# Expert stage of a decoder layer: the dots' normed row in a PSUM bank, similarities in one bank

## Chip, cores, metric

One NeuronCore of a Trainium2 chip runs the whole kernel. The metric is the device time of one execution in microseconds (us), less being better. The engines are PE (matmul), DVE (vector), ACT (scalar), POOL (GpSimd) and SP, which here only issues DMAs.

## The reference

A decoder layer on x of 8 x 224 tokens with 512 features, fp32: self-attention with 16 heads, cross-attention over 750 context rows, and a product-key mixture of experts. Only the last is touched by the change; its core is

```python
q = jnp.einsum('bnd,de->bne', x, w_q)            # then batch norm over all tokens
sim = jnp.einsum('pbnhd,hkpd->pbnhk', q, keys)   # two halves p, 8 heads h, 128 keys k
sx, ix = jax.lax.top_k(sim[0], TOPK); sy, iy = jax.lax.top_k(sim[1], TOPK)
...                                              # top 8 of the 64 sums, indices ix*128 + iy
wd = down_embed[indices]; wu = up_embed[indices]
h = gelu_new(jnp.einsum('bnd,bnhkd->bnhk', x, wd))
h = jax.nn.softmax(scores, axis=-1) * h
out = jnp.einsum('bnhk,bnhkd->bnd', h, wu)
```

with x the layer-normed rows. Every token takes 8 experts in each of 8 heads, and an expert has a down row and an up row of 512 numbers.

## The kernel before

`build_attention` does both attentions batch by batch and leaves x2 in `acc` and its layer norm in `xn_all`, both token-major: 14 tiles (`NTF`) of 128 tokens. `build_experts` then runs the 8 heads (`HF`).

**Units.** A head has 28 units (`NV`), two per token tile. A unit treats 4 of the 8 chosen experts (`HU`) of each of the tile's 128 tokens. Its steps, by engine and line: POOL gathers 4 times 128 rows of 4 KB (down and up row side by side) into a slot of the ring `rows` of 6 units (L1769); DVE forms 4 dots of the down halves with the tile's normed row, in place, the sum going to `hidden` (L1965); ACT takes the gelu (L2042, `active`); DVE multiplies by the gate (L1976, `weight`); ACT writes 4 diagonal matrices (L2047, `diag`, room for two units); PE multiplies each by the up rows (L1819), and a tile's 8 products accumulate in one of two PSUM banks, `ps_y` or `ps_o`. After every second product `rows_used` counts up, and POOL waits on it before it reuses the slot. DVE adds a finished tile into `acc` two tiles later (L1955, `add_rows`).

**Steps.** The choice of the next heads' experts is cut into 40 steps that are interleaved with the units: `steps_in` says which steps go with which unit. From head 1 on, unit v does step v + 20 of the next head (v < 20) and step v - 8 of the one after (v >= 8). `PE_STEPS`, `DVE_STEPS` and `ACT_STEPS` hold them: PE projects queries (L1789, steps 0 to 7 and 12 to 19) and multiplies them with the keys, two tiles at a time, 7 groups for each half (`match_keys`, L1802, into `ps_t`, steps 12 to 18 and 23 to 29); DVE takes statistics of the queries (L1847), and finds the best 8 of each group (`search`: MAX8 at L1876, FIND_INDEX8 at L1879), two steps behind the product, then joins the halves (L1889 to L1899) and makes indices and gates (L1908 to L1934, steps 32 to 39). ACT normalizes the queries (L2022, steps 10 and 22).

**Order in a unit.** Each engine's queue is in order. PE: steps, then the four products. DVE: dots, `add_rows` on a tile's first unit, steps, wait for the gelu, weight. ACT: gelu, wait for the weight, diagonals, steps. The product of group g waits until search g - 2 is done, as two banks alternate; the search waits for its product through `sims_made`.

**PSUM.** All eight banks are in use: four for projected queries (`ps_s`), two for similarities (`ps_t`, called `ps_m` in `build_experts`), two for the weighted sums.

Of the kernel before, what the change touches and what calls it, by code (L numbers as in the profile page):

```python
# [14 lines left out]
ALU = mybir.AluOpType  # L15
# [59 lines left out]
AHEAD_TILES = (B - 1) * S // P // 2 * 2  # L75
# [1463 lines left out]
HF = 8  # L1539
KD = 128  # L1540
NK = 128
# [19 lines left out]
def build_experts(nc, a, out, x2_dram, x2n_dram, acc, xn_all, xn_t, w_in, keys, gamma, beta, stats, ps_q, ps_m, ps_out, ident):  # L1561
# [5 lines left out]
    with ExitStack() as ctx:  # L1567
# [51 lines left out]
        idx_here = sem("idx_here")  # L1619
        rows_in = [sem(f"rows_in{g}") for g in range(RING)]  # L1620
        rows_used = sem("rows_used")
        hidden_ready = sem("hidden_ready")
        active_ready = sem("active_ready")
        weight_ready = sem("weight_ready")
# [21 lines left out]
        def piece_of(n0, n1):  # L1646
# [3 lines left out]
            match = q_t[:, 0:2 * n * TOP * TOP].rearrange("p (s t k j) -> p s t k j", s=2, k=TOP, j=TOP)  # L1650
            return pair, match

        def group(g):
            return range(g * TPB, min(NTF, (g + 1) * TPB))

# [3 lines left out]
        for half, (p0, m0) in enumerate(((0, 12), (12, 23))):  # L1659
            for i in range(2 * QC):  # L1660
                PE_STEPS[p0 + i].append(("project", half, i))
            for c in range(QC):
                DVE_STEPS[p0 + 2 * c + 3].append(("count", half, c))
            DVE_STEPS[p0 + 10].append(("affine", half, 0))
            for g in range(NG):
                PE_STEPS[m0 + g].append(("match", half, g))
                DVE_STEPS[m0 + g + 2].append(("search", half, g))
        for k, part in ((32, 0), (33, 1), (34, 2), (35, 3)):
            DVE_STEPS[k].append(("pairs", 0, part))
        for k, part in ((36, 0), (36, 1), (37, 2), (38, 3), (39, 4)):  # L1670
# [103 lines left out]
        def _(pe):  # L1774
# [19 lines left out]
            def match_keys(head, half, g):  # L1794

                n = nth(head, half)
                pe.wait_ge(q_ready, QC * n + -(-P * TPB * (g + 1) // QN))

                if n >= 1 or g >= 2:
                    pe.wait_ge(searched, NG * n + g - 1)  # L1800
                for i in group(g):
                    mm = nc.tensor.matmul(ps_m[g % 2][:, (i % TPB) * NK:(i % TPB + 1) * NK],  # L1802
                                          q_t[:, i * P:(i + 1) * P], keys[:, half, :], start=True, stop=True)
                mm.then_inc(sims_made, 1)

# [38 lines left out]
        def _(dve):  # L1844
# [22 lines left out]
            def search(head, half, g):  # L1867
# [2 lines left out]
                dve.sem_inc(passed_dve, 1)  # L1870

                def sims(i):
                    return ps_m[g % 2][:, (i % TPB) * NK:(i % TPB + 1) * NK]

                for i in group(g):
                    nc.vector.max(best[:, half, i, :], sims(i))  # L1876
# [80 lines left out]
            def unit(h, t, s, step):  # L1957
                v = SPT * t + s
                b = v % 2
                if h == 0 and v == SPT * AHEAD_TILES:  # L1960
                    dve.wait_ge(x2_in, 32)
                dve.wait_ge(rows_in[v % RING], 16 * HU * (uses(v % RING) * h + v // RING + 1))
                for k in range(HU):
                    down = rows[:, v % RING, k, 0:D]
                    last = nc.vector.tensor_tensor_reduce(down, down, xn_all[:, t, :], 1.0, 0.0, ALU.mult, ALU.add,  # L1965
                                                          hidden[:, b, k:k + 1])
                last.then_inc(hidden_ready, 1)
                if v == 0 and h >= 1:
# [41 lines left out]
        def _(act):  # L2010
# [18 lines left out]
            def steps(head, k):  # L2029
                for stage, half, part in ACT_STEPS.get(k, ()):  # L2030
# [4 lines left out]
                    else:  # L2035
                        soften(head)

            def unit(h, t, s, step):
                v = SPT * t + s
                b = v % 2  # L2040
                act.wait_ge(hidden_ready, NV * h + v + 1)
                nc.scalar.activation(active[:, b, :], hidden[:, b, :], ACT.Gelu_apprx_tanh).then_inc(active_ready, 1)  # L2042
                act.wait_ge(weight_ready, NV * h + v + 1)

                act.wait_ge(rows_used, 2 * (NV * h + v - ND + 1 + RING))
                for k in range(HU):
                    nc.scalar.activation(diag[:, HU * (v % ND) + k, :], ident[:], ACT.Copy, scale=weight[:, b, k:k + 1])\  # L2047
                        .then_inc(diag_ready, 1)
                step()
# [7 lines left out]
                    soften(0, n0, n1)  # L2057

            first_head()
            run_heads(steps, unit, lambda: None)  # L2060


# [69 lines left out]
```

## Time and profile before

| | us |
|---|---|
| median of 3 runs | 2746.43 (2737.4 to 2747.01) |
| the profiled execution | 2732.75 |
| its span | 2730.9 |
| granted TensorE clock, mean | 0.943 of full speed |
| first gather starts | 1358.2 |

The profile is a page on one execution: busy time by engine, the span in 40 slices, DMA queues, the chain of waits that ended last, the costliest groups of instructions with what ended the idle time before them, and DMA issues. Behind the page, the trace can be asked for a stretch, a line, a tile, the waits or the order in time. Lines are those of the kernel file (L1965). In a timeline row the numbers are start and duration in us; the bracket at its end is the engine's idle time before it and what ended it, where "issue" stands for nothing that the profile shows and "remote" or "an unknown queue" for a releaser that it can't name. In the order of work, `ps_y` and `ps_o` at L1819 are the weighted sums of alternate tiles.

### The profile page before, as it was taken

What the parts mean: (1) busy time and instruction counts of PE and PEld (TensorE: products, weight loads), DVE (VectorE), ACT (ScalarE), POOL (GpSimd) and SP (SyncE); (2) the same over time, 40 slices, a digit from 0 to 9 for tenths busy, and PEclk for the clock granted to TensorE, in tenths of its full rate; (3) what the DMA queues carried; (4) which work ended last, traced back from release to release, by engine and by line L of the source; (5) the groups of instructions that cost most, each with busy time, mean ns of one, the idle gap of its engine ahead of it and who ended that gap; (6) DMA issues with size and microseconds to landing.
All of it is one profiled execution on the core that took longest, in us unless ns stands there. A gap on an engine that the chain in (4) does not pass through costs nothing.

```text
span 2730.9 us, 37792 instructions
## 1 busy us (share of the span) xinstructions
PE 2356.3 (86%) x12444; PEld 1259.1 (46%) x12444; DVE 1869.2 (68%) x5474; ACT 1176.5 (43%) x3224; POOL 1144.1 (42%) x1082
## 2 busy tenths in 40 slices
PE   8999999999999999998868888778878788876767
PEld 4565555656555565655534433333333343332323
DVE  4676777777687777768467767677775766766554
ACT  3365574736557473657223423323333332332222
POOL 3111212111121211120166576676667666577665
PEclk9999999999999999999989999989899998898889
DMA  4001001010100101011189899999999999899998
GB/s 175 30 1 37 8 8 37 1 44 1 41 4 10 36 1 43 1 60 58 58 320 364 299 369 357 349 354 345 358 352 363 351 362 358 309 359 356 355 375 330
DMA packets 161954, 521.78 MB, mean 191 GB/s; under 512 B 17248, under 2 KB 27488, under 8 KB 161760
## 3 DMA queue, kind: packets, MB, share of 16 engines
q0 software_dynamic: 129024, 469.82, 45.8%
q1 hardware_dynamic: 31152, 48.03, 5.3%
q8 instruction: 100, 1.64, 0.2%
q10 hardware_dynamic: 1584, 1.52, 0.2%
q14 instruction: 94, 0.77, 0.1%
HBM read 508.30 MB, written 11.01 MB: 190 GB/s over the span
## 4 chain that ended last, share of the span: by engine, by line
PE 20%; issue 10%; DVE 10%; another core or an unknown queue 3%; POOL 3%; DMA 3%; ACT 1%; DVEq 1%; POOLq 0%; ACTq 0%
PE ps_y L1819 7%; PE ps_o L1819 7%; DVE e_rows L1965 5%; PE ps_s L1789 3%; POOL e_rows L1769 3%; DMA e_rows<-in_experts,e_idx 3%; PE ps_t L1802 1%; ACT e_diag L2047 1%; DVE acc L1955 1%; DVE e_at L1899 1%; DVE e_best_at L1879 1%; DVEq L1903 0%; DVE q_stats L1847 0%; ACT e_q_t L2022 0%
## 5 line engine op out<-in xcount | busy, mean ns | idle before, releaser
L1769 POOL DMA_INDIRECT e_rows<-in_experts,e_idx x896 | 908.6, 1014 | 473.0 <-issue 284.6
L1965 DVE CUSTOM_DVE_ANT_0 e_rows<-e_rows,xn_all 128x512 f32<-128x512 f32 x896 | 568.6, 688 | 148.4 <-DMA e_rows<-in_experts,e_idx 112.5
L1819 PE MATMUL ps_o<-e_rows,e_diag 128*128 128x512 f32 x896 | 443.1, 642 | 149.2 <-issue 131.3
L1819 PE MATMUL ps_y<-e_rows,e_diag 128*128 128x512 f32 x896 | 434.5, 632 | 121.6 <-ACT e_diag L2047 60.4
L2047 ACT ACTIVATE e_diag<-ident_f,e_weight 128x128 f32<-128x128 f32 x896 | 286.3, 390 | 560.5 <-DVE e_weight L1976 197.1
L1819 PEld LDWEIGHTS ps_o<-e_rows,e_diag 128*128 128x128 f32 x896 | 179.8, 206 | 384.7 <-issue 362.5
L1819 PEld LDWEIGHTS ps_y<-e_rows,e_diag 128*128 128x128 f32 x896 | 178.1, 203 | 355.1 <-issue 316.1
L1133 DVE SCALAR_TENSOR_TENSOR ring<-ps_s,mask 112x750 f32<-112x750 f32 x248 | 225.0, 936 | 129.2 <-PE ps_s L624 110.1
L1359 ACT ACTIVATE ring<-ring,neg_max 112x750 f32<-112x750 f32 x248 | 226.8, 916 | 157.6 <-DVE neg_max L1143 157.2
L1143 DVE CUSTOM_DVE_ANT_0 ring<-ring,mask_bias 112x750 f32<-112x750 f32 x248 | 233.5, 989 | 0.0
L2042 ACT ACTIVATE e_active<-e_hidden 128x4 f32<-128x4 f32 x224 | 45.6, 204 | 359.5 <-DVE e_hidden L1965 143.3
L1789 PE MATMUL ps_s<-xn_t,w_in 128*128 128x448 f32 x464 | 196.7, 550 | 0.0
L1377 ACT COPY prob_t<-ps_t 125x336 f32<-125x336 f32 x400 | 160.5, 443 | 83.4 <-PE ps_t L639 75.6
L639 PE MATMUL ps_t<-ident,ring 112*125 112x112 f32 x1164 | 178.2, 284 | 7.1 <-ACT prob_t L1377 6.0
L1485 POOL TENSOR_TENSOR x_b<-x,bo 112x1024 f32<-112x1024 f32 x8 | 18.9, 2358 | 391.9 <-DVE xn_t L1079 389.9
L561 PE MATMUL ps_y<-w_v,xn_t 128*125 128x512 f32 x384 | 178.1, 603 | 4.1 <-DVE v_c L973 4.1
L639 PEld LDWEIGHTS ps_t<-ident,ring 112*125 112x125 f32 x1164 | 152.2, 192 | 52.8 <-issue 32.2
L484 PE MATMUL ps_y<-xn_t,xn_all 128*128 128x375 f32 x424 | 146.1, 487 | 0.0
L1336 ACT ACTIVATE ring<-ring,neg_max 112x112 f32<-112x112 f32 (+1 forms) x256 | 108.7, 427 | 72.9 <-DVE neg_max L1045 72.7
L1475 POOL TENSOR_TENSOR rstd<-var_eps,minus_half 112x1 f32<-112x1 f32 (+1 forms) x24 | 16.4, 684 | 276.4 <-DVE var_eps L874 276.4
L457 PE MATMUL ps_y<-acc,act_t 128*112 128x512 f32 x280 | 129.4, 600 | 1.6 <-DVE xn_t L903 1.6
L624 PE MATMUL ps_s<-k_t,q_t 32*112 32x375 f32 x1024 | 117.2, 527 | 8.4 <-DVE ring L1133 7.5
(226 smaller groups left out, 3189.8 us busy)
## 6 DMA issues: line engine op xcount, KB each, us to landing
e_rows<-in_experts,e_idx POOLq DMA_INDIRECT x896
xn_t<-in_ctx_t SPq DMA_DIRECT2D x8, 1500.0 KB, 6.7
w_in<-in_ffn_wq SPq DMA_DIRECT2D x16, 256.0 KB, 7.6
acc<-in_x SPq DMA_DIRECT2D x8, 448.0 KB, 4.9
acc<-x_dram SPq DMA_DIRECT2D x7, 512.0 KB, 6.5
xn_all<-x2n_dram SPq DMA_DIRECT2D x7, 512.0 KB, 7.1
out<-acc SPq DMA_DIRECT2D x14, 256.0 KB
x_dram<-x SPq DMA_DIRECT2D x7, 448.0 KB, 3.1
```

The costliest lines, as they stand in the source:

```text
L484: mm = nc.tensor.matmul(out[:, 0:HC], w_k[:, kc, c * P:(c + 1) * P], ctx_t[:, kc, part * HC:(part + 1) * HC], start=(kc == 0), stop=(kc == ...
L561: mm = nc.tensor.matmul(ps_y[0:CT, :], ctx_t[:, kc, j * CT:(j + 1) * CT], w_v[:, kc, :], start=(kc == 0), stop=(kc == KC - 1))
L639: mm = nc.tensor.transpose(out[0:CT, j * TT:(j + 1) * TT], cross_rows(b, u, 1)[:, 0, o:o + CT], ident[0:TT, 0:TT])
L1133: nc.vector.scalar_tensor_tensor(cross_rows(b, u, 2)[:, :, cols], ps_s[pair][0:TT, :, 0:HC], 1.0 / SQRT_HD, spread(mask[:, t, cols], 1, 2) ...
L1143: nc.vector.tensor_tensor_reduce(row, row, mask_bias[:, t, :], -1.0, 3.4e38, ALU.add, ALU.min, neg_max[:, u:u + 1]).then_inc(cs_shifted.se ...
L1359: nc.scalar.activation(row, row, ACT.Exp, bias=neg_max[:, u:u + 1], scale=-1.0, accum_out=row_sums[:, 1, t * H + h:t * H + h + 1]).then_in ...
L1377: nc.scalar.copy(prob_t[0:CT, u % 4, i * HB:(i + 1) * HB], turn_bank[turn_place(2 * u + i)][0:CT, :])\
L1769: pool.indirect_dma_start(rows[:, v % RING, k, :], None, table[:, :], bass.IndirectOffsetOnAxis(ap=idx[:, e:e + 1], axis=0))\
L1789: mm = nc.tensor.matmul(q_bank(head, half, c)[:, 0:QN], w_q[:, half, kc, :], xn_t[:, kc, c * QN:(c + 1) * QN], start=(kc == 0), stop=(kc = ...
L1819: mm = nc.tensor.matmul(ps_out[t % 2][:], diag[:, HU * (v % ND) + k, :], rows[:, v % RING, k, D:], start=(s == 0 and k == 0), stop=(s == S ...
L1965: last = nc.vector.tensor_tensor_reduce(down, down, xn_all[:, t, :], 1.0, 0.0, ALU.mult, ALU.add, hidden[:, b, k:k + 1])
L2047: nc.scalar.activation(diag[:, HU * (v % ND) + k, :], ident[:], ACT.Copy, scale=weight[:, b, k:k + 1])\
```

## The change

The tile's normed row no longer comes to the dots from `xn_all` in SBUF. ACT copies it into the PSUM bank `ps_m[1]` (`rows_here`), one copy per tile and head, 112 in all: after the gelu of a tile's second unit it copies the row of the next tile, and counts up `xn_here`; DVE waits for that before the first dot of each tile. The first copy is made ahead of head 0, once all 14 searches of head 0 are done, since these still use both banks. From head 1 on, similarities have only `ps_m[0]`. The product of group g then waits for search g - 1, and the search stands one step behind the product in `DVE_STEPS` in place of two. The wait for the edge tiles of `xn_all` (`x2_in`) moves from DVE to ACT.

```diff
--- before.py
+++ after.py
@@ -1619,6 +1619,7 @@
         idx_here = sem("idx_here")
         rows_in = [sem(f"rows_in{g}") for g in range(RING)]
         rows_used = sem("rows_used")
+        xn_here = sem("xn_here")
         hidden_ready = sem("hidden_ready")
         active_ready = sem("active_ready")
         weight_ready = sem("weight_ready")
@@ -1649,6 +1650,12 @@
             pair = q_t[:, 0:n * TOP * TOP].rearrange("p (t x y) -> p t x y", x=TOP, y=TOP)
             match = q_t[:, 0:2 * n * TOP * TOP].rearrange("p (s t k j) -> p s t k j", s=2, k=TOP, j=TOP)
             return pair, match
+
+        xn_here_at = ps_m[1]
+
+        def sims_bank(head, g):
+
+            return ps_m[g % 2] if head == 0 else ps_m[0]
 
         def group(g):
             return range(g * TPB, min(NTF, (g + 1) * TPB))
@@ -1664,7 +1671,7 @@
             DVE_STEPS[p0 + 10].append(("affine", half, 0))
             for g in range(NG):
                 PE_STEPS[m0 + g].append(("match", half, g))
-                DVE_STEPS[m0 + g + 2].append(("search", half, g))
+                DVE_STEPS[m0 + g + 1].append(("search", half, g))
         for k, part in ((32, 0), (33, 1), (34, 2), (35, 3)):
             DVE_STEPS[k].append(("pairs", 0, part))
         for k, part in ((36, 0), (36, 1), (37, 2), (38, 3), (39, 4)):
@@ -1796,10 +1803,12 @@
                 n = nth(head, half)
                 pe.wait_ge(q_ready, QC * n + -(-P * TPB * (g + 1) // QN))
 
-                if n >= 1 or g >= 2:
+                if head >= 1:
+                    pe.wait_ge(searched, NG * n + g)
+                elif n >= 1 or g >= 2:
                     pe.wait_ge(searched, NG * n + g - 1)
                 for i in group(g):
-                    mm = nc.tensor.matmul(ps_m[g % 2][:, (i % TPB) * NK:(i % TPB + 1) * NK],
+                    mm = nc.tensor.matmul(sims_bank(head, g)[:, (i % TPB) * NK:(i % TPB + 1) * NK],
                                           q_t[:, i * P:(i + 1) * P], keys[:, half, :], start=True, stop=True)
                 mm.then_inc(sims_made, 1)
 
@@ -1870,7 +1879,7 @@
                 dve.sem_inc(passed_dve, 1)
 
                 def sims(i):
-                    return ps_m[g % 2][:, (i % TPB) * NK:(i % TPB + 1) * NK]
+                    return sims_bank(head, g)[:, (i % TPB) * NK:(i % TPB + 1) * NK]
 
                 for i in group(g):
                     nc.vector.max(best[:, half, i, :], sims(i))
@@ -1957,12 +1966,12 @@
             def unit(h, t, s, step):
                 v = SPT * t + s
                 b = v % 2
-                if h == 0 and v == SPT * AHEAD_TILES:
-                    dve.wait_ge(x2_in, 32)
+                if s == 0:
+                    dve.wait_ge(xn_here, NTF * h + t + 1)
                 dve.wait_ge(rows_in[v % RING], 16 * HU * (uses(v % RING) * h + v // RING + 1))
                 for k in range(HU):
                     down = rows[:, v % RING, k, 0:D]
-                    last = nc.vector.tensor_tensor_reduce(down, down, xn_all[:, t, :], 1.0, 0.0, ALU.mult, ALU.add,
+                    last = nc.vector.tensor_tensor_reduce(down, down, xn_here_at[:], 1.0, 0.0, ALU.mult, ALU.add,
                                                           hidden[:, b, k:k + 1])
                 last.then_inc(hidden_ready, 1)
                 if v == 0 and h >= 1:
@@ -2035,11 +2044,21 @@
                     else:
                         soften(head)
 
+            def rows_here(h, t):
+
+                if h == HF:
+                    return
+                if h == 0 and t == AHEAD_TILES:
+                    act.wait_ge(x2_in, 32)
+                nc.scalar.copy(xn_here_at[:], xn_all[:, t, :]).then_inc(xn_here, 1)
+
             def unit(h, t, s, step):
                 v = SPT * t + s
                 b = v % 2
                 act.wait_ge(hidden_ready, NV * h + v + 1)
                 nc.scalar.activation(active[:, b, :], hidden[:, b, :], ACT.Gelu_apprx_tanh).then_inc(active_ready, 1)
+                if s == SPT - 1:
+                    rows_here(h + (t + 1) // NTF, (t + 1) % NTF)
                 act.wait_ge(weight_ready, NV * h + v + 1)
 
                 act.wait_ge(rows_used, 2 * (NV * h + v - ND + 1 + RING))
@@ -2057,6 +2076,8 @@
                     soften(0, n0, n1)
 
             first_head()
+            act.wait_ge(searched, 2 * NG)
+            rows_here(0, 0)
             run_heads(steps, unit, lambda: None)
```

## Rows read from the trace of the kernel before

**Rows 1.** The page's busy table: busy us, share of the span, instructions.

```profile
PE 2356.3 (86%) x12444; PEld 1259.1 (46%) x12444; DVE 1869.2 (68%) x5474; ACT 1176.5 (43%) x3224; POOL 1144.1 (42%) x1082
```

**Rows 2.** Busy time by stretch; then the page's DMA row for gathers (software queue).

```profile
1391.00:2731.00 1340.00, 1063.42 (x2600) 485.06 (x2600) 899.69 (x3269) 421.73 (x1239) 897.33 (x894) 0.90 0.94 351
...
q0 software_dynamic: 129024, 469.82, 45.8%
```

**Rows 3.** Page's group of gathers; then their line: durations min/median/max, POOL's waits.

```profile
L1769 POOL DMA_INDIRECT e_rows<-in_experts,e_idx x896 | 908.6, 1014 | 473.0 <-issue 284.6
...
L1769 POOL DMA_INDIRECT e_rows<-in_experts,e_idx x896: 935/941/1826, 1358.2 to 2714.4; - x180
...
  PE ps_y L1819: 74.6, 40
  remote: 56.7, 26
  PE ps_o L1819: 43.9, 33
```

**Rows 4.** DVE's waits in the stage: total us, times, longest.

```profile
DVE e_rows L1965 <- DMA e_rows<-in_experts,e_idx: 112.5, 53, 8.2
```

**Rows 5.** Chain of waits, 1390 to 2731: shares by line, two long pieces.

```profile
by line: issue 20.6%; PE ps_y L1819 15.2%; PE ps_o L1819 14.8%; DVE e_rows L1965 10.8%; another core or an unknown queue 6.2%; PE ps_s L1789 5.8%; POOL e_rows L1769 5.2%; DMA e_rows<-in_experts,e_idx 5.1%; PE ps_t L1802 2.2%; ACT e_diag L20
...
2589.68 9.88 another core or an unknown queue
2655.07 10.06 issue
```

**Rows 6.** Timeline (start, duration in us): a gather beside silent DVE, one beside dots.

```profile
1907.61 0.94 POOL L1769 DMA_INDIRECT e_rows<-in_experts,e_idx  x1 [0.30 <-issue]
...
1913.43 0.16 DVE L1860 TENSOR_TENSOR e_scale<-e_rstd,gamma 128x1 f32<-128x1 f32 x1 [7.53 <-issue]
...
2049.09 0.69 DVE L1965 CUSTOM_DVE_ANT_0 e_rows<-e_rows,xn_all 128x512 f32<-128x512 f32 x1
...
2049.25 1.34 POOL L1769 DMA_INDIRECT e_rows<-in_experts,e_idx  x1 [0.30 <-PE ps_y L1819]
...
2049.70 0.69 DVE L1965 CUSTOM_DVE_ANT_0 e_rows<-e_rows,xn_all 128x512 f32<-128x512 f32 x1
```

**Rows 7.** Dots by their line; then the page-style group of adds from PSUM.

```profile
L1965 DVE CUSTOM_DVE_ANT_0 e_rows<-e_rows,xn_all x896: 677/687/764, 1390.6 to 2722.3; 128x512 f32<-128x512 f32 x180
...
L1955 DVE TENSOR_TENSOR acc<-acc,ps_y 128x512 f32<-128x512 f32 x56 | 38.2, 681 | 12.8 <-issue 6.4 <-remote 5.9
```

**Rows 8.** ACT's copies by shape: groups of the page.

```profile
L2047 ACT ACTIVATE e_diag<-ident_f,e_weight 128x128 f32<-128x128 f32 x896 | 286.3, 390 | 560.5 <-DVE e_weight L1976 197.1
...
L1359 ACT ACTIVATE ring<-ring,neg_max 112x750 f32<-112x750 f32 x248 | 226.8, 916 | 157.6 <-DVE neg_max L1143 157.2
```

**Rows 9.** Timeline: gelu and next dot at a tile change with short step.

```profile
1849.48 0.20 ACT L2042 ACTIVATE e_active<-e_hidden 128x4 f32<-128x4 f32 x1
...
1849.80 0.69 DVE L1965 CUSTOM_DVE_ANT_0 e_rows<-e_rows,xn_all 128x512 f32<-128x512 f32 x1
```

**Rows 10.** Timeline where PE lags: diagonals, searches, products, next dot.

```profile
2044.99 1.28 ACT L2047 ACTIVATE e_diag<-ident_f,e_weight 128x128 f32<-128x128 f32 x4 [1.50 <-DVE e_weight L1976]
...
2047.92 0.49 DVE L1876 MAX8 e_best<-ps_t 128x8 f32<-128x128 f32 x2
...
2048.72 0.61 PE L1802 MATMUL ps_t<-keys,e_q_t 128*128 128x128 f32 x4
...
2050.67 3.60 PE L1819 MATMUL ps_y<-e_rows,e_diag 128*128 128x512 f32 x8
...
2051.55 0.49 DVE L1876 MAX8 e_best<-ps_t 128x8 f32<-128x128 f32 x2
...
2054.11 0.61 PE L1802 MATMUL ps_t<-keys,e_q_t 128*128 128x128 f32 x4
...
2058.44 0.69 DVE L1965 CUSTOM_DVE_ANT_0 e_rows<-e_rows,xn_all 128x512 f32<-128x512 f32 x1 [5.10 <-DMA e_rows<-in_experts,e_idx]
```

## What the change does to the time: a prediction

> **What bounds the kernel now.** The page's busy table comes first: PE is busy for 86% of the span, DVE 68%, ACT 43%, POOL 42% [rows 1], but these are means over two stages. The change touches only the second one, the experts, which runs from the first gather at 1358 us to the end. The view of stretches shows it: in the 1340 us from 1391 us on, PE is busy 1063 us, DVE 900, POOL 897, ACT 422, the DMA engines 94% of the time at 351 GB/s [rows 2]. No engine is full. Four things take turns, so the next question is what each waits for.
>
> POOL issues 896 gathers, four a unit (224 units, two per token tile, 28 per head). One takes 941 ns at the median, 935 at least, 1826 at most, 1014 in the mean, with 0.30 us before the next [rows 3, 6]. So POOL alone needs 896 x 1.31 = 1177 us. The rest of its time is mostly waiting for a slot of the six-unit ring: 74.6 + 56.7 + 43.9 = 175 us, for PE's last reads (the part called remote has an unseen releaser, which I put with them) [rows 3]. The other side: DVE waits 112.5 us, 53 times, for gathered rows to land [rows 4]. When POOL waits, the consumers are late; when DVE waits, the gathers are. The chain of waits over the stage tells how often which side counts: PE's weighted sums 30%, waits with no visible releaser 27% (20.6% issue, 6.2% unknown), the dots 10.8%, POOL's gathers 5.2%, landings 5.1% [rows 5]. The waits without a releaser come as single stalls of up to 10 us. So the stage is mainly PE plus such stalls, and the gathers decide a small part.
>
> **The change part by part.** *Gathers beside dots.* A dot now reads rows (SBUF) and the normed row (SBUF). While DVE is silent for 7.53 us, the gathers run at 0.94 us; a gather that starts at 2049.25 beside a dot that began at 2049.09 takes 1.34 us, which is 0.40 more, about what was left of the dot [rows 6]. I read this as the gather waiting until the dot lets go. The excess over all gathers is 896 x (1.014 - 0.941) = 65 us of POOL's time, the most that can go; a few other DVE instructions with two SBUF inputs share in it and stay. On the chain there are 5.2% of 1340 = 70 us of gathers, so 69 of them, at 0.073 us excess each: **-5 us**. Bounds: 0, if the excess has another cause, and -65, if all of it counted.
> The Trainium skill (SBUF — State Buffer, section Who interferes with whom) says that a VectorE instruction with two SBUF inputs contends with a GpSimd instruction that reads SBUF, and that one with a single SBUF input does not. By that rule the trace's long gathers agree, and the excess goes with the second SBUF input. The same section infers that a two-input VectorE op doesn't hold back the generation of descriptors; by that sentence alone the term would be 0 and the sum 5 us higher. The 1.34 us gather speaks against it.
>
> *The dots themselves.* 896 of them, at 687 ns in the median (677 to 764). The nearest row that reads one operand from PSUM at the same 128x512 shape, the add of a finished tile, takes 681 ns [rows 7]. So the change per dot lies at -6 to about +6 ns, with the longest dot of the trace (77 ns over the median) as a far end. The dots are 10.8% of the chain, 145 us, and follow each other every 0.61 us (2049.09 to 2049.70), so 238 of them: -2 to +2 us, +18 at the far end, taken as **0**.
> The Trainium skill (VectorE: DVE Perf Modes, section The TRN2 errata — SBUF-src ops pay a fixed extra latency per instruction) gives VectorE 58 cycles of fixed cost from SBUF and 120 from PSUM at 0.96 GHz. That speaks against this change: an estimate from these figures is 65 ns more a dot, so 15 us in place of 0 in the sum. Rows 7 show no such step between an add with a PSUM input and a dot without.
>
> *The copy.* ACT gains 112 copies of 128x512 and as many increments; DVE gains 112 waits and loses one (the wait on x2_in moves to ACT). No ACT instruction of the trace writes 512 columns to PSUM. From the rows of 128 columns (390 ns) and 750 columns (916 ns) [rows 8], a column costs 0.846 ns, so 512 cost 0.43 us with no fixed part and 0.72 us with all of it. I take 0.70, as both rows have the fixed part. That is 78 us of ACT, in a stage where it is busy 422 of 1340. Behind the copy on ACT stand the diagonals of the same unit; behind DVE's wait stand the dots of the next tile, the hidden values and everything later. The copy starts when the gelu of the tile's second unit is done. DVE has its steps and the weight product in between, so only tile changes with an empty or short step show it: there the gelu starts at 1849.48 and DVE's next dot at 1849.80 [rows 9]; gelu 0.2 and copy 0.7 would move the dot to about 1850.3, 0.5 us. By the step tables these are units 3 and 19 of seven heads (14) and the 14 tile changes of the last head: 28 x 0.5 = 14 us of DVE's time. DVE's dots are on the chain for 145 us of 616 (896 x 0.687), about a quarter: **+3.5 us**. Bounds: 0 (always hidden by landing rows) and 112 x 0.5 = 56. The first copy waits for the searches of head 0, long before the first dot.
>
> *The search, one step behind.* The number of matmuls and searches is the same, PE's order too, and SP's loads wait for the same products. But the search of a unit now needs the product that PE makes in the unit just before. Where PE multiplies, projects and sums (units 20 to 27), it lags: the diagonals written at 2044.99 are used at 2050.67, 5.7 us later. At 2047.92 DVE searches; its new product is made at 2048.72 and done at 2049.3, so DVE waits 1.5 us. The next search, at 2051.55, needs the product started at 2054.11: with its 0.61 us and the signal DVE is then 3.3 us later than before. It then had 5.10 us to wait for rows anyway [rows 10], so this costs nothing there; PE's own queue isn't held. The price is lead: a stall of DVE or ACT that follows is covered by up to 3.3 us less. With 14 such stretches the bounds are 0 and 46 us; I take one that surfaces: **+3 us**. The case for little: PE, not DVE, is late there.
>
> *One bank.* A product now waits for the search just before it; as the search also moved one step forward, it waits in the same unit as before, and only the second product of each series is newly held, 14 times, by at most its own 0.61 us behind the search: 0 to 9 us, taken as **+1**. Against it: the searches leave unit 28 (the next head's first) and unit 11, which are no longer loaded twice.
>
> **Sum.** -5 + 0 + 3.5 + 3 + 1 = +2.5 us. The profiled execution took 2732.75 us (span 2730.9 and 1.85 around it), so 2735 for it; it stands 13.7 us below the median of 2746.43. On the median: **2749 us**.
>
> **The rivals.** (a) *Faster gathers pay everywhere.* Six units of ring let POOL build up lead that later covers stalls. For it: DVE waits 112.5 us for rows. Against: POOL waits 175 us for the ring, and most of what it saves lengthens these waits; the chain holds only 70 us of gathers; the DMA engines are already 94% busy. Half of the 65 us: -33 + 7.5 = **2721 us**. (b) *The copy becomes the wait, the slower end.* At each tile change DVE waits for ACT, 112 x 0.5 us, if half of it is on the chain: +28 + 3 + 1 - 5, **2773 us**. It decides from the point where ACT is so late that the gelu ends the step in most odd units; ACT's 422 busy us speak against, its stalls for it. (c) *Lost lead.* The search wait surfaces in a third of the stretches: +15 + 3.5 - 5 + 1, **2761 us**. (d) *PSUM costs the dot a fixed time.* Every dot then takes what the longest one takes now, 238 x 0.077 = +18 over the forecast, so **2767 us**. It decides from a mean dot of some 740 ns; the add with a PSUM input speaks against [rows 7]. The Trainium skill's page named at the dots has the rule behind it. (e) *The change doesn't free POOL:* gathers stay at 1014 ns, 0 in place of -5: **2754 us**. (f) *The stalls fall elsewhere.* 27% of the chain, 360 us, is stalls of up to 10 us without a releaser; another instruction stream puts them at other units, where more or fewer are covered. Two stalls more or less on the chain: **2729 or 2769 us**.
>
> **How the numbers follow.** Chances: forecast 0.43, (a) 0.20, (b) 0.10, (c) 0.05, (d) 0.07, (e) 0.05, (f) 0.10, of which 0.04 faster. 0.5%, about what a measurement of this kernel can tell from no change, is 13.7 us, so 2732.7 to 2760.2 is the same. Faster: (a) and part of (f), 0.24. Same: forecast and (e), 0.48. Slower: (b), (c), (d) and the rest of (f), 0.28; (c) lies just over the line. The range takes in (a) down to 2718 and (b) up to 2776, which leaves a deeper gain or a fully exposed copy outside.
>
> **What would show it.** Gathers: mean near 950 ns, minimum unchanged, POOL busy about 55 us less, its ring waits longer by nearly as much. Dots: 681 to 695 ns. Copies: 112 at about 0.7 us, DVE waiting on them for 5 to 20 us in all. Searches: DVE waits on the product (MAX8 behind L1802) 20 to 60 us in all, against few now, while its waits for rows shrink. PE's share of the chain stays above a quarter. It would be wrong if DVE's waits for rows shrink and the ring waits don't grow (then (a)), if dots take 740 ns or more, or if waits on the copy exceed 30 us.

## The result and the profile after

The changed kernel takes **2784.2 us** at the median of 4 runs (2779.3 to 2789.8), the kernel before 2743.4 (2737.4 to 2747.0, 4 runs, one more than in the table ahead): 1.0152 times as long, 95% interval 1.0123 to 1.0181. It is 41 us slower; forecast was 2749, and 2784 lies outside the range of 2718 to 2776. The profiled execution took 2789.75 us (span 2788.0). The two profiled executions lie 57 us apart, 16 more than the medians, so differences between the two traces are somewhat too large for the 41 us.

The page's busy table after, to be laid beside [rows 1]:

```profile
span 2788.0 us, 38015 instructions
PE 2378.2 (85%) x12444; PEld 1270.0 (46%) x12444; DVE 1865.5 (67%) x5474; ACT 1229.8 (44%) x3336; POOL 1080.7 (39%) x1082
```

POOL is busy 63 us less than before, ACT 53 more (the copies), DVE 4 less. Nothing here explains a longer run, so the next view is the stretch of the expert stage, as in [rows 2] (busy us and count of PE, weight loads, DVE, ACT, POOL; granted clock, DMA share, GB/s):

```profile
1391.00:2788.00 1397.00, 1082.33 (x2600) 494.95 (x2600) 898.25 (x3275) 475.03 (x1350) 834.57 (x894) 0.89 0.91 336
```

The stage is 57 us longer than in the profiled execution of before (1397 against 1340). For the same 2600 matmuls PE is busy 19 us more and idle 315 us in place of 277. DVE has the same work and is idle 58 us more. The gathers are not what is late: DMA share and rate fell, and so did DVE's waits for rows (below).

The groups (the gathers of the whole run from the page, the others of the stage: busy us, mean ns, then the idle time in front and what ended it), and the copies by their line (minimum/median/maximum ns, then who waited for them):

```profile
L1776 POOL DMA_INDIRECT e_rows<-in_experts,e_idx x896 | 846.7, 945 | 582.2 <-issue 292.6
L1974 DVE CUSTOM_DVE_ANT_0 e_rows<-e_rows,ps_t 128x512 f32<-128x512 f32 x896 | 563.5, 683 | 117.9 <-DMA e_rows<-in_experts,e_idx 66.6 <-issue 49.3 <-ACT ps_t L2053 1.1
...
L1811 PE MATMUL ps_t<-keys,e_q_t 128*128 128x128 f32 x392 | 69.8, 306 | 136.6 <-remote 47.4 <-issue 46.2 <-DVE e_best_at L1888 43.0
...
L1885 DVE MAX8 e_best<-ps_t 128x8 f32<-128x128 f32 x196 | 48.6, 290 | 192.2 <-remote 133.6 <-issue 31.1 <-PE ps_t L1811 27.4
```

```profile
L2053 ACT COPY ps_t<-xn_all x112: 572/579/594, 1383.2 to 2769.5; 128x512 f32<-128x512 f32 x112
...
who waited for it (us, times):
  DVE e_rows L1974: 1.1, 4
```

What the change aimed at has come: a gather takes 945 ns where it took 1014 [rows 3], a dot 683 where it took 687 [rows 7], and DVE waited 1.1 us in all for the copies. The last two groups stand out: DVE stands 192 us before a search (MAX8), PE 137 us before a product. The waits of before at the same two places (total us, times, longest), first DVE's, then PE's:

```profile
DVE e_best L1876 <- remote: 47.4, 12, 11.5
...
DVE e_best L1876 <- issue: 14.0, 3, 8.6
...
DVE e_best L1876 <- PE ps_t L1802: 7.5, 5, 4.3
```

```profile
PE ps_t L1802 <- DVE e_best_at L1879: 9.6, 8, 4.6
PE ps_t L1802 <- remote: 9.4, 2, 5.6
PE ps_t L1802 <- issue: 4.9, 1, 4.9
```

So 69 us became 192 and 24 became 137. Much of it is only moved. DVE waits 67 us for rows where it waited 112 [rows 4], and PE's waits ahead of the weighted sums that have no visible releaser fell from 187 us to 92, before and then after:

```profile
PE ps_o L1819 <- issue: 131.3, 29, 14.2
...
PE ps_y L1819 <- issue: 56.0, 16, 11.8
```

```profile
PE ps_o L1828 <- issue: 63.3, 24, 9.3
...
PE ps_y L1828 <- issue: 28.3, 16, 5.1
```

PE stands 113 us more before products, but in the whole stage only 38 us more (277 to 315). A longer wait at one place isn't yet the loss; the time that a wait costs has to come from experiments. POOL's waits for the ring grew from 175 us [rows 3] to 276, in the changed kernel's POOL waits:

```profile
POOL e_rows L1776 <- PE ps_y L1828: 136.4, 59, 11.2
POOL e_rows L1776 <- remote: 77.2, 26, 6.0
POOL e_rows L1776 <- PE ps_o L1828: 62.8, 45, 6.6
```

These are 101 us more, 63 of them being the time that POOL no longer spends on gathers. The timeline of the changed kernel shows what one such wait looks like (start, duration, instruction, idle time in front):

```profile
2469.46 0.68 PE L1811 MATMUL ps_t<-keys,e_q_t 128*128 128x128 f32 x4 [1.77 <-issue]
...
2470.48 3.67 PE L1828 MATMUL ps_y<-e_rows,e_diag 128*128 128x512 f32 x8 [0.34 <-issue]
...
2472.53 0.08 DVE L1974 DVE_READ_ACCUMULATOR2_ANT e_hidden<- 128x1 f32 x1
...
2480.42 0.20 ACT L2059 ACTIVATE e_active<-e_hidden 128x4 f32<-128x4 f32 x1 [9.21 <-issue]
2480.53 0.58 ACT L2053 COPY ps_t<-xn_all 128x512 f32<-128x512 f32 x1
...
2487.53 0.50 DVE L1885 MAX8 e_best<-ps_t 128x8 f32<-128x128 f32 x2 [14.92 <-remote]
...
2488.71 0.68 DVE L1974 CUSTOM_DVE_ANT_0 e_rows<-e_rows,ps_t 128x512 f32<-128x512 f32 x1
2488.83 1.28 ACT L2066 ACTIVATE e_diag<-ident_f,e_weight 128x128 f32<-128x128 f32 x4 [7.72 <-DVE e_weight L1985]
2488.88 1.19 PE L1811 MATMUL ps_t<-keys,e_q_t 128*128 128x128 f32 x4 [14.73 <-issue]
```

DVE has stood 14.9 us before its search and PE 14.7 us before its next product: both stand at once. By the order of the program, DVE's search needs PE's product of the unit before, PE's next product needs this search, and ACT's diagonals need DVE's weights behind the search. But the row doesn't show PE's work holding DVE: the product that the search needs has its recorded end at 2470.14, DVE's last dot is done at 2472.6, and the search starts 15 us later. ACT's gelu, which needs only the dots, starts 7.8 us after them. So DVE and ACT stand here for something that the trace doesn't name, and PE has nothing to do until the search is done. Before the change it would have needed a search in this same unit too. Of the 20 waits above 3.5 us before a search in this trace, 16 end 3.9 to 17.4 us after the recorded end of the last product. What the shorter distance costs is therefore left to the experiments.

### The profile page after: what moved, and what is told of

Read it like the earlier page. It is cut to its first block, busy times and chain, and to the rows that moved or that the text cites. A ratio compares the mean times of both kernels' runs of the same rounds, so it can differ in the third digit from the quotient of the medians.

```text
span 2788.0 us, 38015 instructions
## 1 busy us (share of the span) xinstructions
PE 2378.2 (85%) x12444; PEld 1270.0 (46%) x12444; DVE 1865.5 (67%) x5474; ACT 1229.8 (44%) x3336; POOL 1080.7 (39%) x1082
## 4 chain that ended last, share of the span: by engine, by line
PE 17%; DVE 15%; issue 9%; another core or an unknown queue 6%; ACT 2%; DVEq 1%; DMA 1%; POOL 1%; POOLq 0%; ACTq 0%
DVE e_rows L1974 8%; PE ps_o L1828 6%; PE ps_y L1828 6%; PE ps_s L1796 4%; DMA e_rows<-in_experts,e_idx 1%; PE ps_t L1811 1%; ACT e_diag L2066 1%; DVE acc L1964 1%; DVE e_best_at L1888 1%; POOL e_rows L1776 1%; DVE e_at L1908 1%; DVE e_top L1902 1%; DVE e_best L1885 1%; DVEq L1912 0%
## 5 line engine op out<-in xcount | busy, mean ns | idle before, releaser
L1776 POOL DMA_INDIRECT e_rows<-in_experts,e_idx x896 | 846.7, 945 | 582.2 <-issue 292.6
L1974 DVE CUSTOM_DVE_ANT_0 e_rows<-e_rows,ps_t 128x512 f32<-128x512 f32 x896 | 563.5, 683 | 117.9 <-DMA e_rows<-in_experts,e_idx 66.6
L1828 PE MATMUL ps_y<-e_rows,e_diag 128*128 128x512 f32 x896 | 448.0, 649 | 95.6 <-ACT e_diag L2066 67.1
L1828 PE MATMUL ps_o<-e_rows,e_diag 128*128 128x512 f32 x896 | 435.1, 632 | 98.4 <-issue 63.3
L1828 PEld LDWEIGHTS ps_y<-e_rows,e_diag 128*128 128x128 f32 x896 | 184.4, 210 | 337.0 <-issue 305.2
L1811 PE MATMUL ps_t<-keys,e_q_t 128*128 128x128 f32 x448 | 79.2, 307 | 142.4 <-remote 47.4
L1885 DVE MAX8 e_best<-ps_t 128x8 f32<-128x128 f32 x224 | 55.4, 289 | 211.0 <-remote 139.5
L1811 PEld LDWEIGHTS ps_t<-keys,e_q_t 128*128 128x128 f32 x448 | 72.0, 213 | 199.9 <-issue 194.4
```

What stands on the lines that cost most here:

```text
L1776: pool.indirect_dma_start(rows[:, v % RING, k, :], None, table[:, :], bass.IndirectOffsetOnAxis(ap=idx[:, e:e + 1], axis=0))\
L1811: mm = nc.tensor.matmul(sims_bank(head, g)[:, (i % TPB) * NK:(i % TPB + 1) * NK], q_t[:, i * P:(i + 1) * P], keys[:, half, :], start=True, ...
L1828: mm = nc.tensor.matmul(ps_out[t % 2][:], diag[:, HU * (v % ND) + k, :], rows[:, v % RING, k, D:], start=(s == 0 and k == 0), stop=(s == S ...
L1974: last = nc.vector.tensor_tensor_reduce(down, down, xn_here_at[:], 1.0, 0.0, ALU.mult, ALU.add, hidden[:, b, k:k + 1])
```

## The experiments

The lead theory was this: not the copy, the dots or the gathers cost time, but the new distance. A search one step behind and one bank let PE and DVE hold each other within a unit, so a stall of one engine isn't worked off by the other. (The product waits for a search in its own unit before and after; what changed is that the search now needs the product of one unit before instead of two.) Rivals: the copy on ACT; the dot's new source; stalls falling elsewhere by chance.

All runs fall into two groups. In some sessions (a session is a set of kernels run side by side on one chip) the kernel before takes 2743 to 2753 us, as here, and the traces have many waits without a visible releaser; in others it takes 2585 us, and they have hardly any. I call them **A** and **B**; each experiment is compared with the kernel before in its own session.

**Parts of the change without stalls (B, before 2585.3).** One kernel has the bank and the step of the change, but dots from SBUF and no copy (it is called the coupling below; its edit is shown beside the change, cut at "..."); one has the step alone, with both banks:

```diff
-                    dve.wait_ge(xn_here, NTF * h + t + 1)
-                    ... tensor_tensor_reduce(down, down, xn_here_at[:], ...
+                    ... tensor_tensor_reduce(down, down, xn_all[:, t, :], ...
-                if s == SPT - 1:
-                    rows_here(h + (t + 1) // NTF, (t + 1) % NTF)
```

```diff
 (beside before, the step alone)
-                DVE_STEPS[m0 + g + 2].append(("search", half, g))
+                DVE_STEPS[m0 + g + 1].append(("search", half, g))
```

> One part alone: similarities in one bank from head 1 on and the search one step behind; the dots still read the normed row from SBUF, and there is no copy. Lead theory (the product and the search hold each other within one unit, so a stall of PE or of DVE can no longer be covered by the other's work): at least the whole loss of the change, 40 to 50 us above before, since the relief of the gathers is missing; DVE's waits before MAX8 near 190 us in the expert stage against 69 in before, gathers still at 1014 ns. Gather theory (faster gathers or the PSUM operand are what costs): within 10 us of before. Copy theory (ACT's extra work costs): within 10 us of before.

> The search one step behind the product, but both banks kept (a product waits for search g - 2). Lead theory, with the wait of DVE for PE as its main half: 15 to 35 us above before. If the single bank (PE waiting for the search just before) is the main half: within 10 us of before. Copy and gather theories: within 10 us of before.

Measured: bank and step together 2594.2 us, 1.0038 (1.0025 to 1.0051), +8.9; the step alone 2591.9, 1.0028 (1.0018 to 1.0037), +6.6. Both cost something where there are no stalls; the two intervals overlap, so the bank's own share isn't told apart here. The lead theory had expected 40 to 50 us for the first and 15 to 35 for the second. It got 8.9 and 6.6, about a fifth of the 41 us at most, in a session of the other kind than that of the result.

The third kernel is before plus the copy and the waits on it, the target being a tile in SBUF; banks and steps are those of before:

```diff
+        xn_here_at = sb("xn_here_at", [P, D])
+                if s == 0:
+                    dve.wait_ge(xn_here, NTF * h + t + 1)
+                nc.scalar.copy(xn_here_at[:], xn_all[:, t, :]).then_inc(xn_here, 1)
```

> The copy, its semaphore and DVE's wait on it as in the change, but into a tile in SBUF from which the dots read; both banks and two steps as in before. Lead theory: within 8 us of before (the copy is hidden), gathers still at about 1014 ns. Copy theory: 20 to 45 us above before. Theory that another instruction stream puts the stalls elsewhere: anything within 20 us of before on either side, since 112 copies and 112 waits are added.

Measured: 2586.2 us, 0.9999 (0.9990 to 1.0009). The copy and its wait cost nothing; its line in this kernel, with DVE's wait of 3.1 us:

```profile
L2051 ACT COPY e_xn_here_at<-xn_all x112: 601/602/618, 1373.5 to 2566.8; 128x512 f32<-128x512 f32 x112
...
  DVE e_rows L1972: 3.1, 9
```

The fourth kernel is the change with the distance given back: while the query projections don't need their last bank, the odd groups' products go there, so 11 of a head's 14 products and searches have two banks and two units again. The three around groups 5 and 6 of the first half stay coupled.

```diff
+        def lent(half, g):
+            return g % 2 == 1 and (half == 1 or g < 5)
         def sims_bank(head, half, g):
-            return ps_m[g % 2] if head == 0 else ps_m[0]
+            return ps_m[g % 2] if head == 0 else ps_q[QC - 1] if lent(half, g) else ps_m[0]
+        def search_step(half, g):
+            return g + 1 if half == 0 and g in (4, 5, 6) else g + 2
-                DVE_STEPS[m0 + g + 1].append(("search", half, g))
+                DVE_STEPS[m0 + search_step(half, g)].append(("search", half, g))
```

> The change with the coupling taken away for 11 of 14 products of a head: the bank of the fourth block of projected queries, idle at that time, takes the odd groups, so the product waits for search g - 2 and the search is two steps behind; groups 5 and 6 of the first half stay coupled. Dots from PSUM and copies as in the change. Lead theory: most of the 41 us comes back, -15 to +10 us against before; gathers at 945 ns, DVE's waits before MAX8 below 110 us. Gather or copy theory: stays 25 to 45 us above before.

Measured: 2586.3 us, 1.0001 (0.9991 to 1.0011). The small loss of B is gone with the distance given back, while PSUM dots and copies stay. It also shows what the faster gathers are worth on B, in the stretch from 1391 us, first in the kernel with the SBUF copy, then in this one:

```profile
1391.00:2585.00 1194.00, 1031.36 (x2599) 466.24 (x2597) 893.46 (x3248) 474.11 (x1345) 874.27 (x888) 0.97 1.00 392
```

```profile
1391.00:2585.00 1194.00, 1027.71 (x2600) 465.92 (x2600) 890.15 (x3254) 474.70 (x1349) 836.34 (x890) 0.98 1.00 393
```

POOL is busy 38 us less, and the time is the same: the DMA engines are busy for all of it, at 392 and 393 GB/s. That the full DMA engines are why the gain doesn't show is argued, not shown.

**Stalls put in on purpose (B, before 2585.2).** First the changed kernel itself. Then three kernels with the same dummy work in them, so that their times are longer by it: in every head ten products of 512 columns (some 8.6 us of PE) in units 4 and 22, and 13 statistics of 512 columns (some 7.8 us of DVE) in units 7 and 25. From head 1 to the last but one, products stand in units 3 to 9 and 20 to 26, so the stalls are put where the distance matters. One is before, one the change, one the change with the lent bank.

```diff
+                if v in (4, 22):
+                    for _ in range(10):
+                        nc.tensor.matmul(ps_out[t % 2][:], xn_t[:, 0, 0:P], xn_t[:, 0, 0:D], start=True, stop=True)
...
+                if v in (7, 25):
+                    for j in range(13):
+                        nc.vector.bn_stats(held[:, j, :], xn_all[:, 0, :])
```

> The changed kernel itself once more, beside before on the chip of the experiments. If this chip again shows before near 2585 us with hardly any waits without a releaser, the lead theory (the coupling costs where PE and DVE stall) expects 0 to 12 us above before, as the coupling alone gave 10 us there, less up to 5 us for the gathers. A theory in which the coupling costs by itself, stalls or not, expects 35 to 45 us. If before is near 2743 us, both expect 35 to 45 us.

> Before with stalls put in by hand: in every head 10 dummy products (about 8.6 us of PE) ahead of the sums of units 4 and 22, and 13 statistics of a constant row (about 7.8 us of DVE) before the steps of units 7 and 25. It is the base for the two kernels beside it. Whole time: 40 to 200 us above before, as some of the 8 x 33 us is covered. No theory on the change depends on its size.

> The changed kernel with the same stalls put in. Lead theory: clearly more over s1_before_held than the changed kernel is over before without stalls, 20 to 60 us more. Theory that the loss belongs to the coupling whatever stalls, or to the copy: the same distance as without stalls, within 6 us.

> The changed kernel with the lent bank (11 of 14 products uncoupled) and the same stalls. Lead theory: within 10 us of s1_before_held. Otherwise it stays with s2_after_held.

Measured: the change without stalls 2595.2, 1.0040 (1.0027 to 1.0054), +9.9. With stalls: before 2661.5 (1.0296), change 2696.5 (1.0428), lent bank 2660.7 (1.0291). The same stalls cost before 76 us and the change 101: its loss grows from 9.9 to 35.0 us, and the lent bank's is -0.8. The waits at the two places, DVE's and then PE's, in the order before, change, lent bank, all with stalls:

```profile
DVE e_best L1880 <- PE ps_t L1803: 17.3, 6, 10.0
```

```profile
PE ps_t L1803 <- DVE e_best_at L1883: 25.0, 7, 5.0
```

```profile
DVE e_best L1889 <- PE ps_t L1812: 115.8, 34, 9.1
```

```profile
PE ps_t L1812 <- DVE e_best_at L1892: 64.5, 20, 5.8
```

```profile
DVE e_best L1905 <- PE ps_t L1828: 30.4, 13, 10.2
```

```profile
PE ps_t L1828 <- DVE e_best_at L1908: 21.4, 6, 4.7
```

The releasers have names here, as the stalls are known: DVE waits for PE's product and PE for DVE's search, 180 us in all against 42 and 52. In the changed kernel all 16 search waits above 3.5 us end 0.14 to 0.15 us after the product's recorded end: here the search does stand for PE, unlike in the A trace of the change. The stalls stand at the same units in all three, so the rival of stalls falling elsewhere doesn't explain this 35 us. This shows how two engines at a short distance hold each other when a stall is PE's or DVE's own; that the unseen stalls of A act the same way isn't shown.

**Step and bank apart, with these stalls.** The step alone and the coupling (step and bank), on A (before 2752.8), beside the lent bank without stalls:

> Both banks, the search one step behind, dots from SBUF, with the stalls put in. If the wait of DVE for PE (search one step behind) is the main half of the loss under stalls: 20 to 35 us above the 2661.5 of s1_before_held. If the single bank is: within 10 us of it.

> One bank and the search one step behind, dots from SBUF and no copy, with the stalls put in. Lead theory: as s2_after_held, 2697 within 6 us, since copy, PSUM operand and faster gathers are worth nothing here. If faster gathers or the copy had a share under stalls: more than 8 us away from 2697.

> The changed kernel with the lent bank once more, to see it where before takes 2743 us, should this chip be of that kind. Lead theory: within 12 us of before on either kind of chip. Otherwise 30 to 45 us above before where before is near 2743, and within 6 us where it is near 2585.

Measured: step alone 2835.5, coupling 2889.6, so 54 us for the bank with both kinds of stalls at once (before with stalls wasn't among them). The two expectations named times of a B session, so they can't be held against these. The lent bank without added stalls took 2760.4, 1.0027 (0.9997 to 1.0057), where the change has 1.0152: on A too most of the loss (some 33 of 41 us, across two sessions) goes with the distance.

On B (before 2584.6), with before as the base:

> Before with the stalls put in, as the base for the two beside it on the same chip.

> Search one step behind, both banks, stalls put in. If the wait of DVE for PE is the main half: more than half of the distance from s7_before_held to s9_coupling_held. If the single bank is: less than a third of it.

> Both halves of the coupling, dots from SBUF, no copy, stalls put in. Lead theory: 30 to 45 us above s7_before_held where before is near 2585, as the whole change was (35); 50 to 90 us above it where before is near 2750.

> The coupling alone without stalls put in. Lead theory: 35 to 50 us above before where before is near 2750, 10 us where it is near 2585. If copy or PSUM operand had a share of the loss: below 30 us where before is near 2750.

Measured: before 2654.1 (the median of three runs; a fourth took 3540 us and is left out), step alone 2684.7 (+30.6), coupling 2709.0 (+24.3 more, +54.9 in all); coupling without stalls 2597.2, 1.0045 (1.0029 to 1.0061). With stalls both halves cost clearly more than without. The waits tell what each does. With the step alone DVE waits 97 us for products and PE not once for a search; with the bank too, PE waits 68 us for searches:

```profile
DVE e_best L1880 <- PE ps_t L1803: 97.2, 32, 9.6
```

```profile
DVE e_best L1886 <- PE ps_t L1809: 122.5, 34, 9.6
```

```profile
PE ps_t L1809 <- DVE e_best_at L1889: 68.4, 20, 5.5
```

These +54.9 exceed the 30 to 45 us that were expected, and the +35.0 of the whole change with stalls in another B session. Do the faster gathers give 20 us back when there are stalls to recover from? Change and coupling side by side, with stalls, and the coupling without (A, before 2750.3):

> The whole change with the stalls put in, beside s11. If faster gathers pay under stalls: 8 to 20 us below s11_coupling_held. If they are worth nothing there: within 5 us of it.

> Coupling alone (no copy, dots from SBUF) with the stalls put in: 110 to 125 us above before where before is near 2585.

> Coupling alone without stalls put in: 10 to 13 us above before where before is near 2585; 41 to 60 us above it where before is near 2750, if faster gathers also give something back there.

Measured: change 2894.1, coupling 2890.4, so the gathers give nothing back here (the difference of 3.7 is within the intervals, 1.0471 to 1.0541 and 1.0457 to 1.0557). Whether they do on B, where the 20 us were seen, wasn't run side by side. The coupling without stalls took 2769.6, 1.0068 (1.0043 to 1.0094), +19.2. That misses what the lead theory had expected of it on A, 35 to 50 us in one expectation and, should the faster gathers pay, 41 to 60 in another; below 30 was named as the sign that copy or PSUM operand has a share of the loss. Its waits for the product, then those of the lent bank on A (both with no stalls added):

```profile
DVE e_best L1882 <- remote: 128.2, 20, 14.7
...
DVE e_best L1882 <- PE ps_t L1808: 39.1, 29, 2.8
...
DVE e_best L1882 <- issue: 23.6, 6, 9.4
```

```profile
DVE e_best L1901 <- remote: 36.6, 13, 9.2
...
DVE e_best L1901 <- issue: 19.5, 11, 7.0
...
DVE e_best L1901 <- PE ps_t L1827: 17.7, 9, 5.4
```

191 us against 74: the coupling alone brings the searches' wait to the change's 192, and the lent bank brings it back near before's 69. The same wait goes with 19 us in the one kernel and 41 in the other, so its length doesn't give the loss.

**What stays open.** On A the distance is worth 19 us when its loss is added to before alone, and some 33 when it is given back to the whole change; the change costs 41. The intervals of coupling and change (up to 1.0094, from 1.0123) don't meet, and the two weren't run in one session of A without added stalls (the changed kernel's repeat fell on B). Copy, dots and gathers cost nothing measurable on B, and with stalls on A the two kernels are equal, so I have no cause for the other 22 us. The traces say where they lie, not why: the stage of the change has PE busy 18 us more than that of the coupling (1082 against 1064) for the same 2600 matmuls, and idle only 4 us more (315 against 310). The lent bank's PE is busy 1077 us (the last two in the rows below, coupling first), and it was 1063 before. So the two A kernels with copy and PSUM dots have the slower matmuls, at a mean granted clock of 0.89 against 0.90. But one kernel's PE time varies nearly as much: 1033 us and 1045 for the coupling on B, in two sessions, at 0.97 and 0.96. Whether the slower PE is cause, consequence or chance isn't shown.

```profile
1391.00:2765.00 1374.00, 1064.45 (x2600) 488.66 (x2600) 899.50 (x3275) 423.00 (x1239) 886.26 (x894) 0.90 0.92 342
```

```profile
1391.00:2765.00 1374.00, 1076.66 (x2600) 492.29 (x2600) 900.57 (x3275) 473.95 (x1350) 837.07 (x894) 0.89 0.91 342
```

Also open is what the waits without a releaser are, and how a shorter distance makes more of them show before the searches. No kernel here beat the one before; the lent bank equals it within 0.1% on B.

## Why the prediction was wrong

**What bounds the kernel** was read rightly in kind: the stage is PE plus stalls, the gathers decide little. The use made of it was not: having put 27% of the chain down to single stalls [rows 5], the working priced the change's new waits in a stretch without one.

**Gathers, -5.** The mechanism was right: mean 945 ns (near 950 was expected), POOL busy 63 us less (55), the ring waits longer by more than that (101). The gain itself is nowhere to be seen: on B the change, 2595.2 against 2585.2, and the coupling without the relief, 2594.2 and 2597.2 against 2585.3 and 2584.6, cost about the same. The gathers are shorter on B too: mean 949 ns in the change, 1000 in the coupling. On the rule of the Trainium skill (SBUF — State Buffer, section Who interferes with whom): the gathers got shorter when the dot lost its second SBUF input, so the trace agrees with the rule. The section's inference, that a two-input operation leaves the generation of descriptors alone, can't be carried over to a whole gather: 69 ns of it went with that operand. No row tells reading its indices from making its descriptors.

**Dots, 0.** Right: 683 ns, within the 681 to 695 named. The 65 ns more a dot worked out from the Trainium skill (VectorE: DVE Perf Modes, section The TRN2 errata — SBUF-src ops pay a fixed extra latency per instruction) show neither in the dot's duration nor between dots: they follow each other every 0.60 to 0.61 us after the change, as before.

**Copy, +3.5.** Too high. It takes 0.58 us, not 0.70, and DVE waited 1.1 us for it, 4 times, not 5 to 20 us. The tile changes with a short step [rows 9] were a real place, but counted 28 times where 4 showed up. The rival that made it the bound (2773) fell with the kernel that has only the copy: 0.9999.

**The search, one step behind, +3: the step that failed.** It was priced at one stretch in which PE lagged by 5.7 us and DVE had 5.1 us of waiting for rows [rows 10]. "PE's own queue isn't held" is right for the step alone (with stalls, PE waits for no search there), but not for the change: with one bank as well, PE's products wait 137 us in place of 24, 43 of them with the search as the named releaser. And the lead lost isn't "up to 3.3 us" for one stall. The search lost a whole unit of distance, and since the product already needed a search of its own unit, the two engines now hold each other within one unit. A wait can then be as long as the stall behind it, not as the lag of a calm stretch. The stalls put in on B show this in the waits; on A, where most long search waits outlast the product by 4 us and more, it rests on the times of the kernels alone. The list of what to look for expected 20 to 60 us before searches "against few now"; it is 192 against 69, and those 69 were in the trace of before, unread, as was a stall of 14.2 us ahead of PE's sums. Measured, the step costs 6.6 us without stalls and 30.6 with those put in; step and bank together cost 19 us on A, where the sum had 4.

**One bank, +1: the same error.** "It waits in the same unit as before" is a right reading of the steps, with 9 us at most as the price. Without stalls the bank's share is too small to tell (8.9 against 6.6, with intervals that overlap); with them it is 24.3, as PE's product again waits for a search of its own unit, and that search is now itself held by PE. The bound of 9 was a duration of the product; it should have been the length of a stall. The two bounds together, 46 and 9, would have held the 41 us; the slowest case made of these terms, rival (c), took 15 of the 46.

**The rivals.** (c), the lost lead, had the mechanism, with a chance of 0.05 and 2761 us. The lent bank shows the distance to be the main part of the loss, though added alone it gives under half of it; the size (a third of 14 stretches) was too small. (a), (b) and (d) fell; (b)'s number, 2773, is nearer to 2784 than any other, but DVE waited 1.1 us for the copies, so that is no merit of its mechanism. (e) fell in its premise, since POOL was freed, but its size was right: that gain was 0. (f) isn't needed for the larger part; whether it has to do with the 22 us left I can't say. PE's share of the chain was to stay above a quarter; all PE lines have 32.0%, the weighted sums alone 23.7% (38.0% and 30.0% before), and the dots went from 10.8% [rows 5] to 16.4%. The chain of the changed kernel's stage:

```profile
by line: issue 18.0%; DVE e_rows L1974 16.4%; PE ps_o L1828 12.5%; PE ps_y L1828 11.2%; another core or an unknown queue 10.9%; PE ps_s L1796 5.9%; DMA e_rows<-in_experts,e_idx 2.9%; PE ps_t L1811 2.4%; ACT e_diag L2066 2.1%; DVE acc L1964 
```

The weighted sums lost 6.3 points and the dots gained 5.6, as one would expect of two engines that take turns instead of running apart, though the chain doesn't prove it; waits without a releaser went from 27% to 29%.

## What to carry to other kernels

A buffer and a step of distance between two engines are there for the stalls of the stage. The same distance was worth 9 us in a calm session, 19 to 33 in one with unseen stalls and 55 with stalls put in. So price its loss against the longest waits in the trace, at every handover, and not against a stretch that happens to be calm. A wait that grows at one place may have left another; only the time, or the idle time of the whole engine, says what it costs. If a change needs the bank of such a pair, look first for one that is idle at that time: here a lent bank took all of the loss back on B and most of it on A. And relief for an engine that waits for a ring goes into that wait first.

## What the runs showed of the hardware

The same kernel before took 2585 us in some sessions and 2743 to 2753 in others. In the traces of the first kind without added stalls (none of them of before unaltered) the expert stage has the DMA engines busy 99 to 100% of the time at 388 to 393 GB/s, hardly any wait on an unseen releaser and a granted clock of 0.96 to 0.98; in the second they are at 0.91 to 0.94 and 336 to 351 GB/s, with such waits up to 15 us long, at a clock of 0.89 to 0.90. What causes it isn't shown, nor whether it belongs to a chip or to the time of the run: the record names chip 10 for a session of B (2585.2) and, some 13 minutes later, for one of A (2752.8). A change that costs 0.4% in the one kind costs 1.5% in the other.

In the second kind, a search of the changed kernel could start 4 to 17 us after the recorded end of the last product (16 of its 20 long waits); with stalls put in on B it was 0.14 to 0.15 us in all 16 long waits.

A copy of 128x512 numbers by ACT took 579 ns into PSUM, on A and on B, and 602 ns from the same source into SBUF (B).
